# Attention pooling on one core: x's low parts move from GpSimd to VectorE

## The reference, cut to what matters

```python
attn_in = jnp.tanh(jnp.einsum('bsd,da->bsa', hidden, W1) + b1)
scores = jnp.einsum('bsa,a->bs', attn_in, v)
mask = jnp.where(pt == 0, prefix_m[None], jnp.where(pt == 1, postfix_m[None], cloze_m[None]))
masked_scores = jnp.where(mask, scores[:, None, :], NEG_INF)
p = jax.nn.softmax(masked_scores, axis=-1)
cnt = jnp.sum(mask, axis=-1).astype(hidden.dtype)
pooled = jnp.einsum('bjl,bld->bjd', p, hidden) / cnt[..., None]
...
xq = act_quant(rmsnorm(x))
```

## Time and profile before

| what | value |
|---|---|
| time, median of 3 executions | 843.38 us (840.73 to 844.75) |
| the profiled execution | 850.21 us, of it a span of 848.3 us |
| PE busy | 746.7 us (88% of the span) |
| DVE busy | 500.0 us (59%) |
| ACT busy | 500.4 us (59%) |
| POOL busy | 344.9 us (41%) |

### The profile page before, as it was taken

How to read it: one execution, slowest core, us unless ns; L and a number is a source line. 1 busy time by engine, 2 the same in 40 slices (tenths; PEclk the granted TensorE clock), 3 DMA queues, 4 the chain that set the end, 5 groups by cost and what they waited for, 6 DMA issues and landing times. The chain is left out here.

```text
span 848.3 us, 10204 instructions
## 1 busy us (share of the span) xinstructions
PE 746.7 (88%) x3504; PEld 474.7 (56%) x3504; DVE 500.0 (59%) x930; ACT 500.4 (59%) x706; POOL 344.9 (41%) x307
## 2 busy tenths in 40 slices
PE   6885799998999999456999999965699999999996
PEld 3333577776777777334677777753244444444442
DVE  2396155544544554133466555532789999999993
ACT  1253146653577788234655665632678888888883
POOL 0205606526245212223455554422245555555554
PEclk9997999999999999767999999987999999999999
DMA  6998849887558466431111120000012222222221
GB/s 202 315 398 299 291 176 339 293 295 215 169 140 207 153 147 149 55 126 51 50 50 51 51 83 17 1 0 21 19 61 63 75 75 76 70 68 75 75 69 68
DMA packets 41699, 109.00 MB, mean 128 GB/s; under 512 B 5392, under 2 KB 6176, under 8 KB 38448
## 3 DMA queue, kind: packets, MB, share of 16 engines
q1 hardware_dynamic: 33712, 94.84, 31.7%
q0 software_dynamic: 7424, 13.06, 8.5%
q10 hardware_dynamic: 512, 0.45, 0.2%
HBM read 88.59 MB, written 28.13 MB: 138 GB/s over the span
## 5 line engine op out<-in xcount | busy, mean ns | idle before, releaser
L1354 PE MATMUL ps<-ff_q,qt 128*128 128x512 bf16 x512 | 123.1, 386 | 4.6 <-PEq L993 3.1
L1378 PE MATMUL ps<-ff_q,ht 128*128 128x512 bf16 x512 | 117.9, 384 | 0.0
L898 PE MATMUL ps<-w_h,inner_l 128*128 128x512 f32 x256 | 104.0, 406 | 7.9 <-DVE inner_l L849 7.6
L719 POOL DMA_INDIRECT x_after_experts<-y,row_of_slot x32 | 51.4, 1607 | 145.5 <-DVE y L837 110.7
L899 PE MATMUL ps<-w_l,inner_h 128*128 128x512 f32 x256 | 102.0, 398 | 0.0
L900 PE MATMUL ps<-w_h,inner_h 128*128 128x512 f32 x256 | 101.9, 398 | 0.0
L1418 DVE SCALAR_TENSOR_TENSOR h<-ps,scale,bias 128x1024 f32<-128x1024 f32 x64 | 81.5, 1279 | 16.9 <-PE ps L1354 16.9
L786 ACT ACTIVATE inner_h<-ps 128x512 fp32r<-128x512 f32 x64 | 38.0, 594 | 90.4 <-PE ps L888 65.1
L849 DVE SCALAR_TENSOR_TENSOR inner_l<-ps,inner_h 128x512 fp32r<-128x512 f32 x64 | 44.2, 690 | 79.7 <-ACT inner_h L786 66.6
L1378 PEld LDWEIGHTS ps<-ff_q,ht 128*128 128x128 bf16 x512 | 50.6, 99 | 62.0 <-issue 3.5
L1397 ACT ACTIVATE h<-h,to_q 128x2048 int8<-128x2048 f32 x32 | 64.2, 2005 | 34.2 <-DVE to_q L1455 34.2
(11 more groups left out here) (222 smaller groups left out, 1450.8 us busy)
## 6 DMA issues: line engine op xcount, KB each, us to landing
w_in_sb<-in_w_in_t SPq DMA_DIRECT2D x8, 2048.0 KB
w_raw<-in_w_out_t SPq DMA_DIRECT2D x16, 1024.0 KB
raw<-in_ff_t SPq DMA_DIRECT2D x16, 1024.0 KB
x_after_experts<-in_x SPq DMA_DIRECT2D x8, 1024.0 KB
x_sum<-x_after_experts SPq DMA_DIRECT2D x8, 1024.0 KB, 4.9
x<-x_after_experts SPq DMA_DIRECT2D x32, 256.0 KB, 2.7
out<-res SPq DMA_DIRECT2D x32, 256.0 KB, 2.0
x_sum<-in_x_t SPq DMA_DIRECT2D x6, 1024.0 KB, 6.6
```

The lines of the kernel that those rows point to most:

```text
L898: pe.matmul(ps[:, s, :], inner_l[:, k % 2, c], w_h[:, k % RING, :], start=k == 0, stop=False)
L1354: m = pe.matmul(ps[:, f, :], qt[:, t, k, :], ff1_q[:, k, f * 512:(f + 1) * 512], start=k == 0, stop=k == KD - 1)
L1378: mm = pe.matmul(ps[:, OUT[t3 % 2], :], ht[:, t3 % 2, k // 2, k % 2, :], ff2_q[:, k, :], start=k == 0, stop=k == KF - 1)
```

## The change

GpSimd no longer computes `x_l`; the two subtractions of 128x1024 elements are issued by VectorE in a new helper `x_low`, called behind `low_part(b1, (0, 1))`. GpSimd's waits for `x_h` and for the pooled blocks of two batches ago go with them. TensorE gets one wait at the head of its part of the stage, for the attention's weights.

```diff
                         if inside(b := i - 1, BATCH):
-                            pool.wait_ge(x_h_cp, b + 1)
-                            if b >= 2:
-                                pool.wait_ge(pooled, TPB * (b - 1))
                             kd = pool.value_load(at_i[0:1, 2, b:b + 1], min_val=0, max_val=2)
                             for half in (0, 1):
-                                ts = slice(2 * half, 2 * half + 2)
-                                pool.tensor_tensor(x_l[:, b % 2, ts, :], x_sum[b % 2][:, ts, :],
-                                                   x_h[:, b % 2, ts, :].bitcast(F32), ALU.subtract).then_inc(x_l_cp, 1)
                                 if half == 0:
                                     pool.wait_ge(top_ready, b + 1)
...
+                    pe.wait_ge(att_in, 4 * DMA)
                     for i in range(BATCH + LAG):
...
+
+                    def x_low(b):
+                        ve.wait_ge(x_h_cp, b + 1)
+                        for half in (0, 1):
+                            ts = slice(2 * half, 2 * half + 2)
+                            ve.tensor_tensor(x_l[:, b % 2, ts, :], x_sum[b % 2][:, ts, :],
+                                             x_h[:, b % 2, ts, :].bitcast(F32), ALU.subtract).then_inc(x_l_cp, 1)
...
                             low_part(b1, (0, 1))
+                            x_low(b1)
                         if inside(b3, BATCH):
                             keep_q(b3)
```

## The result

| kernel | median | executions | ratio to before (95%) |
|---|---|---|---|
| before | 843.52 us (840.73 to 844.75) | 4 | |
| changed | 849.38 us (847.07 to 850.71) | 4 | 1.0091 (1.0054 to 1.0128) |

The change makes the kernel slower by 5.9 us on the medians, where 8.6 had been forecast; by the ratio it is 7.7 us, and the interval, 4.6 to 10.8 us, holds all three. The execution that was profiled took 847.07 us, with a span of 845.2.

What follows compares the result with a forecast made beforehand. PE's own work was taken to bound the 23.77 us step, with DVE's path to the last greatest equally long. Six steps cost 10.7 us, less 1.9 and 0.2 in the first two: +8.6 on 843.4, 852.0 us, range 845.5 to 860.

Steps and rivals of the forecast that it cites:

- The bound: Pooling step: PE's work fills it, DVE's path is as long; a later last greatest lengthens the step one for one.
- the most that could be gained: Whole kernel: PE's work fills all but 0.24 us of a step, so at most 3.9 us can be gained.
- Six steps: Steps three to eight of the pooling: the last greatest starts 1.79 us late in each, 10.7 us in all.
- The steps ahead of them: First two pooling steps: 1.9 us gained in the first and 0.2 us in the second.
- the freed stall of 1.34 us: DVE's low part 0: no longer held up by POOL's x_l, it ends 1.34 us earlier.
- The price of the operation: Each two-tile subtraction of x on DVE: taken as 1.22 us; 1.38 would add 1.9 us in all.
- keep its turn: Rival, DVE queue: both x_l halves run before mask 3; 1.04 us a step, about +5.5 us, 848.9; chance 0.20.
- the literal form: Shared port: nothing of a blocked instruction done before it is free; about +12.3 us, 855.7; chance 0.48 together with the forecast.
- The collision that stays: DVE's low part 2 still runs into POOL's qt and takes about 2 us.
- The clock: Rival: PE's idle holes halve its clock, 2.3 us a fall, one to six falls, 854 to 866; chance 0.13.
- `x_l` was held up: Rival denied this: mask 3 and x_l run side by side, greatest 0.8 us late, +2.2 us, 845.6; chance 0.09.
- lost the race: Rival "not slower": qt starts over 0.50 us after keep_q, low part 2 goes first; +0.1 us, 843.5; chance 0.07.

Runs made afterwards that it cites:

- Low part last: Kernel before, with POOL keeping both x_l subtractions, the second moved behind the four masks, and qt issued behind to_q: 837.2 us, ratio 0.9912.
- no low parts: Kernel before, with the low parts of x left out from batch 2 on, for POOL and DVE alike: 838.6 us, ratio 0.9921.
- second profile: The changed kernel timed again without edit, beside the kernel before: 856.4 us, ratio 1.0106; also called the second comparison.
- qt late: Changed kernel, with POOL issuing rms first, then waiting for to_q, then issuing its copy qt: 845.1 us, ratio 0.9991 to the kernel before.
- qt late in the kernel before: Kernel before, with only POOL's copy qt moved behind to_q: 843.9 us, ratio 0.9991.
- keep_q first: Changed kernel, with DVE's copy keep_q ahead of the two x subtractions instead of behind them: 861.7 us, ratio 1.0181 to the kernel before.

## Why the prediction was right

- **The bound.** The forecast read from the trace that the path through DVE was as long as the step, so that DVE's lateness would be the step's. The last `greatest` came 1.75 us late in the step that was traced, which grew by 1.76; all six grew by 1.73 to 1.76. Shown.
- **What it had wrong on PE.** The forecast also called 23.77 us PE's own work, said that less than 0.24 us could be taken off a step while that work stays, and put the most that could be gained at 3.9 us. PE was busy for 22.76 us of the step; 0.78 more were a wait for ACT ahead of the projections. "Low part last" took 0.53 us off the step with PE's work unchanged; its stage was 4.3 us shorter and its time 7.4 us below before, and "no low parts" ran at 22.83 us a step. And in the kernel before the last of the six steps took 23.79 us, although PE stood idle for 6.66 of them. So there it was the path through DVE, ACT and POOL that set the step, and not PE. This did not touch the forecast of +8.6 us, since the change made that path longer; it would have misled anyone who asked what was to be gained.
- **The terms.** Six steps cost 10.45 us (from 407.42 to 560.59 against 418.98 to 561.70), forecast 10.7. The steps ahead of them gave back 1.7 us (407.42 - 354.64 = 52.8 against 54.5; 0.9 in the second profile), forecast 2.1. Behind them the last part of the stage took 0.3 us more (0.5 in the second profile), which had no term. The stage came out 9.1 and 10.0 us longer, forecast 8.6. In words the forecast had the freed stall of 1.34 us pay for part of the cost; in the trace the pair of low parts ended 0.05 us sooner within itself, and what paid was DVE's idle time of 1.29 us. Its list of start times had both right.
- **The price of the operation.** No row showed a subtraction of this size on DVE; 1.22 us was taken from a neighbour and 1.21 measured.
- **Who goes first.** This was the open choice. The changed trace settles it: mask 3 (1.99 us) ran between the two subtractions, and the second ended 1.07 us behind it. So DVE did not keep its turn, and that rival falls, although its 848.9 us stood nearer to the first median. The Trainium skill ("SBUF — State Buffer", section "Who interferes with whom") lets the port go to whoever starts first, for a whole instruction; the trace agrees with the order. It does not agree with the literal form, in which nothing of the blocked instruction is done before: the tail behind the other's end was 0.54 us for 128x512 and 1.07 for 128x1024, some 0.14 less than the lengths.
- **The collision that stays.** Low part 2 took 2.00 us beside `qt`, and moving `qt` took 1.33 us from the step. That most of the change's cost needs this collision is shown by the runs "qt late" and "qt late in the kernel before": 0.49 us a step is left without it.
- **The clock.** It stayed at 1.00 in the first five of the six steps, as the forecast had it. The sixth has 0.91, where before has 0.96; there PE stands idle 8.40 us (6.66 before) because no new batch follows, and the step is not lengthened by it (25.54 us). In the run "keep_q first" the clock fell in five steps of six.
- **The other rivals.** `x_l` was held up; `qt` came 0.08 us behind `keep_q`, far from the 0.50 at which it would have lost the race. PE's new wait for the weights was met: its first transpose began 0.19 us behind POOL's first instruction of the stage, where it was 0.04. In "keep_q first", whose `x_l` was later still, the transposes followed block 3 at once, so the later load of x costs nothing.
- **A size that was off.** The time's difference on the first medians was 5.9 us against 8.6 (7.7 by the ratio). The second comparison gave 9, and the stage's length bears the sum out. The other stages differ by 12 us between the two first profiles, more than the whole effect, so how near the first medians came to the forecast is in part luck. What makes them vary was not tried.

Of the expectations behind the prediction two failed in what they were asked for. "keep_q first" missed the clock. "qt late in the kernel before" was to gain 0.24 us a step and gained 0.07: it had the last `greatest` wait for its square, and it stood idle behind low part 3 instead. Two more gave the gain too small: "no low parts" 0.7 us a step against 0.95, and "low part last" 0.6% against 0.9, with its step as expected.

## What to carry to other kernels

Before a subtraction of two tiles is moved from GpSimd to VectorE, draw the two queues side by side: what counts is which instruction stands beside which, since in each pair that met here the later one waited for the rest of the other. Moving one POOL copy by a few us was worth three quarters of what the change cost in a step, and it was worth next to nothing in the kernel where DVE was not late. POOL had an idle place in the same step, behind the masks, and there a new place in its own queue did better than a new engine. And do not call the bottleneck's step its own work before its small waits are taken off: 0.78 us of ACT stood hidden in PE's 23.77.

## What the hardware showed that was not expected

- VectorE and GpSimd took turns, one instruction each. In "keep_q first" four instructions stood against each other, in the order mask 3, subtraction, `qt`, subtraction: POOL's `qt` took 2.88 us instead of 1.90 while DVE's two subtractions took 4.73.
- The granted clock of PE fell behind a wait of 2.53 us, which followed a stretch of transposes and projections, but not behind one of 1.61 us preceded by one of 0.79. The two waits add up to about the same idle time. The fall cost 1.6 us a step. The five falls are of one kernel, and no run varied the length of that wait alone.
